# Summing every fifth row step on GpSimd, as a tree of additions between gathers, instead of on VectorE

## The reference

```python
e = stack([tbl_f[ids[:, f]] for f in range(40)], axis=1)     # 2048 x 40 x 64
viW = einsum('bpd,pde->bpe', e[:, i_idx], W)                 # 780 pairs
z = einsum('bpe,bpe->bp', viW, e[:, j_idx])
h = concatenate([z, dense_ctx], axis=1)                      # 796 wide
h = maximum(h @ W_top1 + b_top1, 0)                          # 512
h = maximum(h @ W_top2 + b_top2, 0)                          # 256
y = h @ W_top3
```

## Time and profile before

| | |
|---|---|
| median of three runs | 1225.1 us |
| the profiled execution's own time | 1221.73 us |
| its span, first to last instruction | 1219.9 us |
| mean granted clock of TensorE | 0.992 of full speed |
| busy: PE / DVE / ACT / POOL | 1156.4 / 972.9 / 879.3 / 606.9 us |
| VectorE's `tensor_reduce` (L698) | 48 instructions, 58.1 us |
| GpSimd's gathers (L521) | 640 instructions |

### The profile page before, as it was taken

One profiled execution on the slowest core, in us unless ns is written; L12 is line 12 of the kernel. 1 busy time (PEld: TensorE's weight loads), 2 busy tenths in 40 slices (PEclk: granted clock), 3 DMA queues, 4 the chain that ended last, 5 costly groups with the idle time before them and its releaser, 6 DMA issues.

```text
span 1219.9 us, 51509 instructions
## 1 busy us (share of the span) xinstructions
PE 1156.4 (95%) x20872; PEld 500.6 (41%) x20872; DVE 972.9 (80%) x850; ACT 879.3 (72%) x6754; POOL 606.9 (50%) x647
## 2 busy tenths in 40 slices
PE   1699999999999999999999999999999999999988
PEld 0256656776433333333343333333334343333333
DVE  0389898999677788999867778999967888899950
ACT  0287977788567688788856677888856777888861
POOL 6776677277773667777755666777720000000000
PEclk9799999999999999999999999999999999999999
DMA  4244444444322323332332223232221221112001
GB/s 136 61 117 132 135 134 131 122 127 125 101 76 78 86 75 82 81 84 61 105 75 75 77 77 97 69 83 82 73 70 60 65 64 54 57 56 72 20 2 47
DMA packets 54342, 101.40 MB, mean 83 GB/s; under 512 B 14420, under 2 KB 14420, under 8 KB 54104
## 3 DMA queue, kind: packets, MB, share of 16 engines
q1 hardware_dynamic: 29520, 67.19, 17.1%
q0 software_dynamic: 20560, 21.34, 9.2%
q10 hardware_dynamic: 4024, 9.58, 2.6%
HBM read 98.05 MB, written 0.01 MB: 80 GB/s over the span
## 4 chain that ended last, share of the span: by engine, by line
PE 69%; issue 9%; DVE 8%; POOL 8%; ACT 3%; DMA 3%; DVEq 0%; ACTq 0%; POOLq 0%
PE u L763 28%; PE zacc L778 14%; PE u L759 13%; PE u L813 8%; POOL gathered L521 6%; DVE prod L689 4%; ACT row_prod L589 3%; DMA gathered<-tbl,index 3%; DVE row_prod L657 3%; PE u L732 2%; PE u L816 2%; POOL first_fields L521 1%; DVE row_prod_v L657 1%; DVE row_sums L698 1%; PE u L819 1%
## 5 line engine op out<-in xcount | busy, mean ns | idle before, releaser
L589 ACT ACTIVATE row_prod<-row_prod 128x64 f32<-128x64 f32 x3328 | 796.3, 242 | 115.6 <-DVE row_prod L657 111.2
L689 DVE TENSOR_TENSOR prod<-u,emb 128x1024 f32<-128x1024 f32 x544 | 642.0, 1218 | 188.3 <-PE u L763 187.1
L589 ACT ACTIVATION_READ_ACCUMULATOR row_prod<-row_prod 128x1 f32 x3328 | 624.8, 188 | 0.0
L521 POOL DMA_INDIRECT gathered<-tbl,index x512 | 484.3, 946 | 215.1 <-issue 141.5
L763 PE MATMUL u<-emb,weights 64*32 64x512 f32 (+1 forms) x10880 | 572.0, 510 | 4.1 <-ACT emb L548 1.2
L763 PEld LDWEIGHTS u<-emb,weights 64*32 64x32 f32 x10880 | 221.4, 107 | 275.4 <-issue 149.2
L778 PE MATMUL zacc<-prod,band 64*32 64x512 f32 (+1 forms) x5240 | 309.0, 505 | 2.2 <-issue 0.9
L759 PE MATMUL u<-weights,emb 64*32 64x512 f32 x4096 | 287.9, 594 | 3.2 <-DVE prod L689 1.2
L657 DVE TENSOR_TENSOR row_prod<-u,first_fields 128x1024 f32<-128x1024 f32 x208 | 253.1, 1217 | 9.1 <-PE u L759 8.2
L778 PEld LDWEIGHTS zacc<-prod,band 64*32 64x32 f32 x5240 | 119.9, 107 | 139.7 <-issue 121.0
L521 POOL DMA_INDIRECT first_fields<-tbl,index x128 | 121.1, 946 | 71.3 <-issue 35.5
(11 more groups left out here) (21 smaller groups left out, 62.7 us busy)
## 6 DMA issues: line engine op xcount, KB each, us to landing
weights<-w_pairs SPq DMA_DIRECT2D x205, 320.0 KB
gathered<-tbl,index POOLq DMA_INDIRECT x512
w12s<-w_top ACTq DMA_DIRECT2D x16, 448.0 KB, 3.4
first_fields<-tbl,index POOLq DMA_INDIRECT x128
w12s<-w_top ACTq DMA_DIRECT2D x8, 256.0 KB, 2.7
index<-ids POOLq DMA_DIRECT2D x1, 320.0 KB, 5.1
z<-dense ACTq DMA_DIRECT2D x4, 32.0 KB
y<-h ACTq DMA_DIRECT2D x4, 2.0 KB
```

The lines of the kernel that those rows point to most:

```text
L521: pool.indirect_dma_start(out=to, out_offset=None, in_=tables[2 * t + e], in_offset=bass.IndirectOffsetOnAxis(ap=index[:, col:col + 1].bit ...
L589: last = nc.scalar.activation(x, x, ACT.Copy, accum_out=row_sums[:, s, q:q + 1])
L689: nc.vector.tensor_tensor(result, products, x, ALU.mult).then_inc(prod_ready, 1)
```

## The change

- The 12 fifth row steps of chunk 0 stay on VectorE. The 36 of chunks 1 to 3 (220, 235, ... 785) are summed by GpSimd. Their products go to a ring of two buffers, `row_prod_o`, in place of `row_prod_v`, and the ring `prod` gives up one buffer (`PRING` 7 to 6).
- GpSimd has no single instruction for it here: it adds the upper half of each run of 64 to the lower half, and repeats this with 32, 16, 8, 4, 2 and 1 numbers (`LEVELS`), six dependent additions over 16 runs, with a semaphore wait between two of them.
- The six additions stand in GpSimd's one program, behind the last gather whose issue step is at most the row step plus one.
- VectorE waits before it writes a buffer of the ring until the sum of two before is done, and `turn_rows` waits for GpSimd's sums.
- `FIELD_STEPS` goes from 3.8 to 4.6, so that gathers are issued later. The last field's issue step moves from 592 to 687, and the transpositions on TensorE move with them.

```diff
-VECTOR_EVERY = 5
+OTHER_EVERY = 5
+OTHER_RING = 2
+LEVELS = (32, 16, 8, 4, 2, 1)
-PRING = 7
+PRING = 6
-FIELD_STEPS = 3.8
+FIELD_STEPS = 4.6
...
+            other = on_pool if c else on_vector
+            (other if r % OTHER_EVERY == OTHER_EVERY - 1 else on_scalar).append(c * N + n)
...
+def make_pool_order():
+    out = [(issue_step(c, q, 2 * t + e), "gather", c, q, t, e) for c, q, t in GATHERS for e in (0, 1)]
+    for x in ON_POOL:
+        place = max([i for i, o in enumerate(out) if o[0] <= x + 1], default=-1) + 1
+        out.insert(place, (x + 1, "reduce", x))
+    return [o[1:] for o in out]
...
+            def reduce_row(at):
+                c, n = divmod(at, N)
+                r = ON_POOL.index(at)
+                pool.wait_ge(prod_ready, at + 1)
+                if at == min(x for x in ON_POOL if x >= c * N):
+                    pool.wait_ge(rows_turned, c)
+                _, t, s = STEPS[c][n]
+                q = 2 * ROW_TILES.index(t) * FF
+                x = row_prod_o[:, r % OTHER_RING, :, :].rearrange("p h (f d) -> p (h f) d", d=DIM)
+                for i, width in enumerate(LEVELS):
+                    if i:
+                        pool.wait_ge(halved, r * (len(LEVELS) - 1) + i)
+                    last = i == len(LEVELS) - 1
+                    to = row_sums[:, s, q:q + 2 * FF].unsqueeze(2) if last else x[:, :, 0:width]
+                    nc.gpsimd.tensor_tensor(to, x[:, :, 0:width], x[:, :, width:2 * width], ALU.add
+                                            ).then_inc(rows_reduced_p if last else halved, 1)
...
+                    elif c * N + n in ON_POOL:
+                        r = ON_POOL.index(c * N + n)
+                        result = row_prod_o[:, r % OTHER_RING, :, :]
+                        if r >= OTHER_RING:
+                            dve.wait_ge(rows_reduced_p, r - OTHER_RING + 1)
...
             def turn_rows(c, b):
                 pe.wait_ge(rows_reduced, reduced_in(c, ON_SCALAR))
                 pe.wait_ge(rows_reduced_v, reduced_in(c, ON_VECTOR))
+                if c:
+                    pe.wait_ge(rows_reduced_p, reduced_in(c, ON_POOL))
```

More of the change, by code:

```diff
@@ L295, in make_reducers @@
 def make_reducers():
-    on_scalar, on_vector = [], []
+    on_scalar, on_vector, on_pool = [], [], []
     for c in range(CHUNKS):
         for r, n in enumerate(ROWS[c]):
-            (on_vector if r % VECTOR_EVERY == VECTOR_EVERY - 1 else on_scalar).append(c * N + n)
-    return on_scalar, on_vector
-ON_SCALAR, ON_VECTOR = make_reducers()
+            other = on_pool if c else on_vector
+            (other if r % OTHER_EVERY == OTHER_EVERY - 1 else on_scalar).append(c * N + n)
+    return on_scalar, on_vector, on_pool
+ON_SCALAR, ON_VECTOR, ON_POOL = make_reducers()
 def reduced_in(c, which):
@@ L407 @@
 ORDER = make_order()
+def make_pool_order():
[4 more added lines that the diff above has]
+    return [o[1:] for o in out]
+POOL_ORDER = make_pool_order()
 USES = [o for o in ORDER if o[0] in ("pairs", "transpose", "turn", "top")]
@@ L435, in pair_tower @@
         row_prod = sb("row_prod", [P, ROW_RING, 2, FF * DIM])
-        row_prod_v = sb("row_prod_v", [P, 2, FF * DIM])
+        row_prod_o = sb("row_prod_o", [P, OTHER_RING, 2, FF * DIM])
         row_sums = sb("row_sums", [P, SUB, ROW_BLOCKS * P])
@@ L464, in pair_tower @@
         rows_reduced_v = sem("rows_reduced_v")
+        rows_reduced_p = sem("rows_reduced_p")
+        halved = sem("halved")
         rows_turned = sem("rows_turned")
@@ L496, in _ @@
             pool.wait_ge(index_loaded, 16)
[L498 to L524, removed]
@@ new lines, in gather @@
+            def gather(c, q, t, e):
+                if e == 0:
+                    if t < FT:
+                        if c >= 2 and t == 0:
+                            pool.wait_ge(prod_ready, (c - 2) * N + ROWS[c - 2][-1] + 1)
+                        if c >= 2:
+                            pool.wait_ge(rows_transposed, TURN_OF[c - 2, t // 2, len(parts(c - 2)) - 1] + 1)
+                    elif RING_USE[c, q, t] >= GRING:
+                        at, part, tile = RING_ORDER[RING_USE[c, q, t] - GRING]
+                        pool.wait_ge(rows_transposed, TURN_OF[at, tile // 2, part] + 1)
+                if issue_step(c, q, 2 * t + e):
+                    pool.wait_ge(prod_ready, issue_step(c, q, 2 * t + e))
+                for s in blocks_of(c, q):
+                    col = (c * SUB + s) * FIELDS + 2 * t + e
+                    if t < FT:
+                        to = first_fields[:, c % 2, s, t * P + e * DIM:t * P + (e + 1) * DIM]
+                        done = first_gathered[t]
+                    else:
+                        to = gathered[:, RING_USE[c, q, t] % GRING, s, e * DIM:(e + 1) * DIM]
+                        done = rows_gathered[RING_USE[c, q, t] % GRING]
+                    pool.indirect_dma_start(
+                        out=to, out_offset=None, in_=tables[2 * t + e],
+                        in_offset=bass.IndirectOffsetOnAxis(ap=index[:, col:col + 1].bitcast(u32), axis=0),
+                    ).then_inc(done, 16)
@@ L526, in _ @@
+            for o in POOL_ORDER:
+                if o[0] == "gather":
+                    gather(*o[1:])
+                else:
+                    reduce_row(o[1])
         @block.scalar
@@ L643, in multiply @@
                         r = ON_VECTOR.index(c * N + n)
-                        result = row_prod_v[:, :, :]
-                        if r:
-                            dve.wait_ge(rows_reduced_v, r)
+                        result = row_prod_o[:, r % OTHER_RING, :, :]
+                        if r >= OTHER_RING:
+                            dve.wait_ge(rows_reduced_v, r - OTHER_RING + 1)
+                    elif c * N + n in ON_POOL:
+                        r = ON_POOL.index(c * N + n)
+                        result = row_prod_o[:, r % OTHER_RING, :, :]
+                        if r >= OTHER_RING:
+                            dve.wait_ge(rows_reduced_p, r - OTHER_RING + 1)
+                        elif r == 0:
+                            dve.wait_ge(rows_reduced_v, len(ON_VECTOR))
                     else:
@@ L692, in reduce_row @@
                 dve.wait_ge(prod_ready, c * N + n + 1)
-                if c and c * N + n == min(x for x in ON_VECTOR if x >= c * N):
-                    dve.wait_ge(rows_turned, c)
                 _, t, s = STEPS[c][n]
                 q = 2 * ROW_TILES.index(t) * FF
-                nc.vector.tensor_reduce(row_sums[:, s, q:q + 2 * FF], row_prod_v[:, :, :].rearrange("p h (f d) -> p (h f) d", d=DIM),
+                r = ON_VECTOR.index(c * N + n)
+                x = row_prod_o[:, r % OTHER_RING, :, :].rearrange("p h (f d) -> p (h f) d", d=DIM)
+                nc.vector.tensor_reduce(row_sums[:, s, q:q + 2 * FF], x,
                                         mybir.AxisListType.X, ALU.add).then_inc(rows_reduced_v, 1)
```

## The result

The changed kernel takes 1227.24 us (median of 20 runs), the kernel before 1225.44 us beside it. The ratio is 1.0021, with a 95% interval of 1.0012 to 1.0029. So the change makes the kernel slower by a fifth of a per cent, where 7.9 us less were forecast. One of the 20 runs of the kernel before took 2958.95 us, which leaves the median as it is. The profiled execution has a span of 1222.7 us against 1219.9.

The account below looks back on a forecast made before the run. TensorE, VectorE and GpSimd were taken as nearly level, each last in some stretches. Terms -2.3 + 0.8 - 4.0 + 1.4 - 2.0 - 1.8 = -7.9 us gave 1213.8, or 1217 us as a median, range 1202 to 1237.

Parts of the forecast that it names:

- step 204's transposition: TensorE, start of chunk 1: its last gather starts near 318 us, not 314.25, so it comes 3.7 us later.
- R: GpSimd's time for one sum of six additions: 1.85 us fixed plus 2.1 us for its numbers, 4.0 us.
- my own slope of 11 us for each us of R: Both saturated stretches grow by 5 and 6 us per us of R; the change breaks even at R = 4.7 us.
- VectorE's relief: Stretches without dense layers: one sum less gives 0.95 us per 15 steps, then TensorE is last; steps 700 to 799 some 5 us less.
- The two stretches where gathers bound: Steps 324 to 399 and 508 to the transposition at 586: GpSimd's fields and sums take 102 and 103 us.
- +0.8: Steps 324 to 424: 102 us stand against 101.2 before, and what follows up to step 424 is unchanged.
- Dense stretches: Nine more sums beside dense layers leave VectorE, at 0.2 us each: -1.8 us.
- The end: The tail of 44.5 us after step 799 stays as it is.
- Ring sizes: PRING 6 and GpSimd's ring of two cost nothing: VectorE's wait is covered, and GpSimd's lateness stays within 30 steps.
- A: Rival: GpSimd becomes the bound through a larger R and the kernel is slower, 1242 us at R 6.3; chance 0.25.
- C: Rival: VectorE and GpSimd block each other's SBUF access, up to 99 us, so about 1316 us; chance 0.02.
- D: Rival: nothing moves, gain and late gathers cancel at R = 4.5 to 4.9, about 1225 us; chance 0.11.

Follow-up runs that it names:

- e1b_pace: The kernel before with FIELD_STEPS 4.6 alone, all sums left on VectorE: 1231.88 us against 1224.26, ratio 1.0059.
- e3b_first38: The changed kernel with 3.8 steps per field for chunk 1 alone, 4.6 after it: 1216.61 us against 1224.26 for the kernel before, ratio 0.9941.
- e8_landing15: e3b_first38 with LANDING 15 instead of 9, placing transpositions later in TensorE's program: 1199.67 us against 1223.45 for the kernel before, ratio 0.9802.
- e7c_pring: The kernel before with PRING 6 instead of 7 alone: 1224.03 us against 1223.45, ratio 1.0006.
- e2c_oldpace: The changed kernel with FIELD_STEPS back at 3.8 throughout: 1263.59 us against 1223.45 for the kernel before, ratio 1.0327.

## Why the prediction was wrong

**The step that failed** is the one on step 204's transposition: "The last of them now starts near 318 us, ... so step 204's transposition comes 3.7 us later: +3.7". The mechanism and the place were right and the term was a third of its size: 3.7 us, where steps 200 to 209 became 11.5 us longer. I counted one field too few. I let field 12 go at step 190 and only field 13 at 194. In the new table field 11 goes at 190, 12 and 13 at 194, 14 and 15 at 195, so all four fields that this transposition needs are queued from 304 us on: 4 x 5.0 = 20 us, and the last of their gathers starts at 323.11. That gives 8.2 us more of waiting. The other 3 us are the clock, which I had not priced: 0.50 through 5.6 us of work gives 2.8 us. This term alone is 7.8 us short, of the 10.7 us between the forecast of -7.9 and the profiled execution's +2.8. e1b_pace shows the stall without the sums, e3b_first38 shows that without it the kernel is faster by 0.6%, at 1216.61 us, where I had forecast 1217.

That agreement is luck. For that kernel my sum has no +3.7 and two transpositions more, -7.9 - 3.7 + 2.2 = -9.4, and R was 3.7 us and not 4.0: by my own slope of 11 us for each us of R that is 3.3 us lower still, some 1212 us.

**What else differed, by the prediction's steps.**

- *R.* The additions take 1288 ns for 512 numbers and 217 ns for 16 on average, so 2.16 ns a number, where I took 2.1, and some 0.18 us fixed, where I took 0.1. The waits between them were 0.08 us each, not the 0.25 us of the earlier trace rows. The Trainium skill's figure (GPSIMD Engine Reference, section 3.1), 4497 ns for 2048 numbers, is 2.2 ns a number; the trace agrees.
- *VectorE's relief.* Right in size. Over the 100 steps from 700 on, the time fell from 122.8 to 117.9 us, where I said some 5. Three steps take 1117.12 - 1113.69 = 3.43 us, TensorE's own pace (timeline of VectorE in the changed kernel, chunk 3):

```profile
1113.69 1.22 DVE L708 TENSOR_TENSOR row_prod<-u,first_fields 128x1024 f32<-128x1024 f32 x1
1114.85 2.35 DVE L740 TENSOR_TENSOR prod<-u,emb 128x1024 f32<-128x1024 f32 x2
1117.12 1.22 DVE L708 TENSOR_TENSOR row_prod<-u,first_fields 128x1024 f32<-128x1024 f32 x1
```

- *The two stretches where gathers bound.* Steps 324 to 399 were forecast at 102 us and took 101.4, and 508 to 583 at 103 and took 101.1. With R at 3.7 my sum gives 100.5 and 101.5, within 1 us of both. The waits are single ones, 4.86 us at step 383 and 4.7 us at step 567. The reason was only half right: e8_landing15 shows that the bound lies in where the transpositions stand, not in GpSimd's throughput.
- *A boundary in the earlier trace rows.* The end of step 399 in the kernel before is at 604.95 us; 606.1 is that of step 400. The two stretches are therefore (columns as in the earlier trace rows):

```profile
504.90:604.95 100.05, 95.61 (x1664) 33.94 (x1650) 92.16 (x82) 84.83 (x661) 74.94 (x80) 1.00 0.32 82
604.95:653.00 48.05, 48.05 (x616) 20.24 (x607) 30.39 (x27) 24.76 (x172) 26.04 (x28) 1.00 0.30 80
```

Against 100.1 us the forecast of 102 is +1.9, not +0.8. Measured, steps 324 to 399 became 1.3 us longer and steps 400 to 424, which I had as unchanged, 1.3 us shorter (46.7). Three smaller slips carry no weight: the 16 fields are issued at steps 324 to 393, not to 388; 76 x 1.143 + 4 x 1.1 is 91.3, not 91.5; and the last fields, from step 602 on, are 19, not 18.
- *Dense stretches.* The -1.8 us did not come. Steps 630 to 639, with a sum and a dense group, took 17.5 us before and 17.9 after: a sum less on VectorE gave nothing there.
- *The end.* It became 1.1 us longer, which I had as unchanged, and is as long in e3b_first38 (45.6 us). The chains that end last differ in one piece, the last 24 sums on TensorE (before, then after):

```profile
1179.63 3.16 PE zacc L778 x24
```
```profile
1181.34 4.27 PE zacc L828 x24
```

The granted clock of the stretch is 0.93 now and was 0.96, so these sums ran for longer at 0.50. Why it fell for longer is not shown.
- *Ring sizes.* `PRING` 6 shows no cost (e7c_pring, 2.2 us at most). GpSimd's ring of two was not tried alone. VectorE's products for it waited 1.6 us in all, 1.5 of them for TensorE, so it held nothing up.

**The rivals.** A, a GpSimd that is slower than I think, had the sign right and the reason wrong: R came out below my value. C is void: the 86 products of VectorE in the changed kernel that run beside an addition for 0.8 us or more take 1218 ns on average, and those that run beside none 1217. The Trainium skill's rule (SBUF — State Buffer, "Who interferes with whom") agrees with this trace. D named the result, about 1225 us, but through a narrow band of R that did not occur. None of the rivals was a table entry that crowds four fields together, and the range of 1202 to 1237 us held the time only since A was in it.

## What to carry to other kernels

When a change moves a table of issue times, list the new entries for the deadline that comes first, one by one, before summing averages: here four entries that met in one place cost more than 36 moved reductions gave back. An engine that is nearly always busy need not be the bound; if it has idle time soon after, moving its consumer's place in the order by a few steps (9 to 15 here) can hide its lateness, and here this was worth more than the change itself (1227 to 1200 us, together with the old pace for one chunk). Price a stall of TensorE with its clock.

## What the runs showed of the hardware

- A wait of 8.9 us took TensorE's granted clock to 0.50, and it stayed there for the first 5.6 us of work, some 3 us of loss on top. Nine waits of 2.0 to 4.3 us (e2c_oldpace) left it at 0.93 over two stretches of 120 us.
- GpSimd's addition of two fp32 tiles takes 1288, 740, 459, 321, 240 and 217 ns for 512, 256, 128, 64, 32 and 16 numbers per partition, and a dependent one starts 0.08 us after the one before it ends (changed kernel, 36 of each).
- The same program took 1225 us in some jobs and 1745 to 1777 us in others, on the same chips in part, with TensorE held up in its small-tile matmuls. The granted clock of the kernel before was 0.93 to 0.96 there and 0.99 to 1.00 elsewhere, which is far from enough for it.
